# Query products of the second attention: one fp32 matmul each, or three over rounded parts and remainders

## What is computed

```python
# x: [32, 32, 512]; 32 heads, NOPE = ROPE = 64, KVR = 32, VD = 128
q = _rmsnorm(x @ wq_a.T, q_a_ln_w) @ wq_b.T
q_nope, q_pe = (q[..., :NOPE], q[..., NOPE:])
ckv_kpe = x @ wkv_a.T
ckv, k_pe = (ckv_kpe[..., :KVR], ckv_kpe[..., KVR:])
kv = _rmsnorm(ckv, kv_a_ln_w) @ wkv_b.T
k_nope, v = (kv[..., :NOPE], kv[..., NOPE:])
q_pe, k_pe = rope(q_pe), rope(k_pe)
scores = (q_nope . k_nope + q_pe . k_pe) * softmax_scale, causal
out = softmax(scores) @ v @ wo.T
```

## Time and profile before

| what | value |
|---|---|
| median of 3 runs | 1026.8 us (1025.46 to 1026.83) |
| the profiled execution's own time | 1021.81 us |
| span of that execution, first to last instruction | 1019.7 us |
| mean granted TensorE clock | 0.991 |
| PE busy | 966.5 us, 95% of the span |
| DVE, POOL, ACT busy | 554.2, 458.9, 229.2 us |
| second attention's stages and output, about 753 to 910 us | 157 us |

### The profile page before, as it was taken

One profiled execution on the slowest core, in us unless ns is written; L12 is line 12 of the kernel. 1 busy time (PEld: TensorE's weight loads), 2 busy tenths in 40 slices (PEclk: granted clock), 3 DMA queues, 4 the chain that ended last, 5 costly groups with the idle time before them and its releaser, 6 DMA issues.

```text
span 1019.7 us, 15772 instructions
## 1 busy us (share of the span) xinstructions
PE 966.5 (95%) x6686; PEld 695.8 (68%) x6686; DVE 554.2 (54%) x947; ACT 229.2 (22%) x443; POOL 458.9 (45%) x417
## 2 busy tenths in 40 slices
PE   6899989999999999999999789989989999899997
PEld 2338877778888788777887578738845556446853
DVE  7856739475384835648376434434147968302323
ACT  4602022221302212111210200110161655500001
POOL 7935548584675837578275403202112434320300
PEclk9999999999999999999999899999999999999999
DMA  5782102011111011211014092694340000072002
GB/s 136 184 238 67 55 1 79 36 42 53 43 73 42 3 50 42 73 42 53 1 42 124 1 215 86 136 195 161 131 186 1 2 2 3 1 158 70 4 1 83
DMA packets 36286, 74.29 MB, mean 73 GB/s; under 512 B 13492, under 2 KB 22260, under 8 KB 33140
## 3 DMA queue, kind: packets, MB, share of 16 engines
q1 hardware_dynamic: 35880, 72.89, 25.6%
q10 hardware_dynamic: 336, 0.39, 0.1%
HBM read 66.26 MB, written 7.01 MB: 72 GB/s over the span
## 4 chain that ended last, share of the span: by engine, by line
PE 72%; DVE 10%; POOL 7%; DMA 4%; ACT 3%; issue 3%; SPq 1%; POOLq 0%; DVEq 0%; ACTq 0%
PE ps L1133 14%; PE ps L1195 12%; PE ps L994 8%; PE ps L1439 5%; PE ps L1267 5%; PE ps L1372 5%; PE ps L1147 4%; POOL w_lo L2307 3%; DVE arena L1973 3%; DMA arena<-level_rows 2%; ACT acts L1484 2%; DVE arena L1970 2%; PE ps L1393 1%; PE ps L1272 1%; PE ps L1399 1%
## 5 line engine op out<-in xcount | busy, mean ns | idle before, releaser
L2413 POOL TENSOR_TENSOR arena<-arena 128x512 f32<-128x512 f32 x80 | 103.5, 1295 | 123.1 <-DVE arena L1973 123.0
L1133 PE MATMUL ps<-xt_hi,w_hi 128*128 128x512 f32 x320 | 127.9, 400 | 5.8 <-POOL w_lo L2307 2.7
L1133 PE MATMUL ps<-xt_lo,w_hi 128*128 128x512 f32 x320 | 125.6, 392 | 0.0
L1133 PE MATMUL ps<-xt_hi,w_lo 128*128 128x512 f32 x320 | 125.0, 391 | 0.0
L1195 PE MATMUL ps<-h_hi,wo_hi 128*128 128x512 f32 x256 | 104.9, 410 | 11.9 <-DVE h_lo L1982 11.9
L1991 DVE TENSOR_TENSOR fresh<-ps,fresh 128x512 f32<-128x512 f32 x56 | 38.7, 692 | 133.7 <-PE ps L1195 133.6
L1973 DVE TENSOR_TENSOR arena<-ps,rope 64x512 f32<-64x512 f32 x160 | 110.2, 689 | 2.2
L1195 PE MATMUL ps<-h_lo,wo_hi 128*128 128x512 f32 x256 | 103.1, 403 | 0.0
L1195 PE MATMUL ps<-h_hi,wo_lo 128*128 128x512 f32 x256 | 102.3, 400 | 0.0
L2330 POOL TENSOR_TENSOR xt<-arena 128x512 f32<-128x512 f32 x24 | 30.5, 1270 | 137.0 <-DVE arena L1878 137.0
L1577 ACT ACTIVATE h_hi<-ps 128x512 fp32r<-128x512 f32 x64 | 33.0, 603 | 203.1 <-PE ps L1180 203.1
(11 more groups left out here) (313 smaller groups left out, 1804.0 us busy)
## 6 DMA issues: line engine op xcount, KB each, us to landing
acts<-in_w_o_dram SPq DMA_DIRECT2D x8, 1024.0 KB, 4.9
arena<-in_a_wo_dram SPq DMA_DIRECT2D x8, 1024.0 KB, 5.7
arena<-kernel_rows SPq DMA_DIRECT2D x11, 512.0 KB, 11.3
acts<-in_w_qkv_dram SPq DMA_DIRECT2D x3, 1792.0 KB, 7.3
acts<-in_w_qkv_dram SPq DMA_DIRECT2D x4, 1280.0 KB, 6.6
w_l<-kernel_rows SPq DMA_DIRECT2D x10, 512.0 KB, 11.9
arena<-level_rows SPq DMA_DIRECT2D x4, 1024.0 KB, 21.3
stream<-in_x_dram SPq DMA_DIRECT2D x4, 512.0 KB, 6.7
```

Source lines behind the costliest of these rows:

```text
L1133: last = pe.matmul(ps[:, bank, :], w[:, r, cols], x, start=(r == 0 and n == 0), stop=(r == R - 1 and n == 2))
L2413: pool.tensor_tensor(qk[:, chunk, half * HALF:(half + 1) * HALF], rot[:, k % 2, 0, :], rot[:, k % 2, 1, :], ALU.add).then_inc(s_rope, 1)
```

## The change

Only the 80 products of L1372 and L1380 and what feeds them are changed. Query input, latent query weights and rotary query weights are each held as a rounded part (float32r) and a remainder, and each product is made in three float32r matmuls that accumulate in one bank: high x high, high x low, low x high. The product of the two remainders is left out. The rounded parts take the place of the float32 tiles that ACT wrote before (`wql_hi`, `qa_hi`); rotary weights, which came by DMA, are rounded by 8 new ACT copies of 128 x 512 and split by 8 new POOL subtractions; the other remainders are made by 4 new DVE instructions from PSUM. `wq_lo` is written over `wq1`. New waits: PE for the DVE remainders and, at the first tile of a stage, for POOL's split; DVE, POOL for ACT's rounding; ACT, before it copies heads out over the weights' place in stages 4 to 7, for query tiles to be done. No DMA is added or moved; one offset is rounded up to a multiple of 8 elements.

```diff
...
@@ -424,9 +425,11 @@
         wo1_last = att1.take(GQ, R * P)
-        wql = att1.take(2, GQ, 4 * LAT)
+        WQL_AT = att1.at
+        att1.take(2, GQ, 4 * LAT)
         wcomb = att1.take(8, R, P)
-        qa_t = att1.take(TOK)
+        QA_AT = att1.at
+        att1.take(TOK)
         keys_t = att1.take(TOK)
         class Wide(Region):
@@ -452,6 +455,12 @@
+        qa_hi = rounded("qa_hi", [P, TOK], "arena", QA_AT)
+        qa_lo = rounded("qa_lo", [P, TOK], "w_l0", 8 * TOK)
+        wql_hi = rounded("wql_hi", [P, 2, GQ, 4 * LAT], "arena", WQL_AT)
+        wql_lo = rounded("wql_lo", [P, 2, GQ, 4 * LAT], "xt", 3 * TOK)
+        wq_hi = rounded("wq_hi", [P, NH // GQ, GQ * 2 * ROT], "w_l0", sp0.at)
+        wq_lo = rounded("wq_lo", [P, NH // GQ, GQ * 2 * ROT], "arena", 0)
         stage1 = acts[:, 0:R * WPART]
...
@@ -1348,6 +1361,7 @@
                     if m % 4 == 3:
                         last.then_inc(s1_turn, 1)
                 pe.wait_ge(s1_wqc, 2)
+                pe.wait_ge(s1_wqlo, 2)
                 for m in range(NTILE):
                     last = pe.transpose(ps[:, 4 + m // 4, (m % 4) * P:(m % 4 + 1) * P],
                                         lat_n[:, m].rearrange("p k l -> p (k l)"), ident[:, :])
@@ -1365,20 +1379,28 @@
                         pe.wait_ge(left, count)
                     return ring1_at[name]
+                def three(bank, high, low, half):
+                    x_hi, x_lo = (x[:, half * HALF:(half + 1) * HALF] for x in (qa_hi, qa_lo))
+                    pe.matmul(ps[:, bank, :], high, x_hi, start=True, stop=False)
+                    pe.matmul(ps[:, bank, :], high, x_lo, start=False, stop=False)
+                    return pe.matmul(ps[:, bank, :], low, x_hi, start=False, stop=True)
                 def queries(i, tiles):
                     for k in tiles:
                         bank = ring(("q", i, k))
                         g, half = k // 2, k % 2
-                        pe.matmul(ps[:, bank, :], wq1[:, GQ * i + g, :],
-                                  qa_t[:, half * HALF:(half + 1) * HALF], start=True, stop=True).then_inc(s1_q, 1)
+                        cols = slice(g * 2 * ROT, (g + 1) * 2 * ROT)
+                        if k == 0:
+                            pe.wait_ge(s1_wlo, i + 1)
+                        three(bank, wq_hi[:, i, cols], wq_lo[:, i, cols], half).then_inc(s1_q, 1)
                 def latent_queries(four):
                     for n in range(8):
                         bank = ring(("l", four, n))
                         g, half = n // 2, n % 2
-                        pe.matmul(ps[:, bank, :], wql[:, four, g, :],
-                                  qa_t[:, half * HALF:(half + 1) * HALF], start=True, stop=True).then_inc(s1_l, 1)
+                        three(bank, wql_hi[:, four, g, :], wql_lo[:, four, g, :], half).then_inc(s1_l, 1)
                 def scores(i):
                     rows = slice(32 * (i % 4), 32 * (i % 4) + 32)
@@ -1415,6 +1437,7 @@
                         last.then_inc(s1_pv, 1)
                 pe.wait_ge(s1_turnc, 6)
+                pe.wait_ge(s1_qlo, 2)
                 pe.wait_ge(s1_wcc, 8)
                 latent_queries(0)
@@ -1626,7 +1649,7 @@
                 def copy_query_weights(q):
                     act.wait_ge(s1_wq, q + 1)
-                    act.activation(wql[:, q].rearrange("p g (i l) -> p g i l", i=4),
+                    act.activation(wql_hi[:, q].rearrange("p g (i l) -> p g i l", i=4),
                                    ps[:, 4 + q, :].rearrange("p (i g l) -> p g i l", i=4, g=GQ), ACT.Copy).then_inc(s1_wqc, 1)
                 def copy_output_weights(i):
@@ -1648,13 +1671,20 @@
                             .then_inc(s1_root, 1)
                 for q in range(2):
                     act.wait_ge(s1_turn, q + 1)
-                    act.activation(qa_t[:, q * HALF:(q + 1) * HALF], ps[:, q, :], ACT.Copy,
+                    act.activation(qa_hi[:, q * HALF:(q + 1) * HALF], ps[:, q, :], ACT.Copy,
                                    scale=a1_ln[:, 0, 0:1]).then_inc(s1_turnc, 1)
                 for q in range(4):
                     act.wait_ge(s1_turn, q + 3)
                     dst = (keys_t, keys_l)[q // 2]
                     act.activation(dst[:, q % 2 * HALF:(q % 2 + 1) * HALF], ps[:, 2 + q, :], ACT.Copy)\
                         .then_inc(s1_turnc, 1)
+                def round_queries(i):
+                    if i == 0:
+                        act.wait_ge(s1_turn, 6)
+                    act.activation(wq_hi[:, i, :], wq1[:, GQ * i:GQ * (i + 1), :].rearrange("p h n -> p (h n)"), ACT.Copy)\
+                        .then_inc(s1_whi, 1)
                 def latents_in(four):
@@ -1687,13 +1717,20 @@
                     last.then_inc(s1_place, 1)
                 def heads_out(i):
+                    if i >= R:
+                        act.wait_ge(s1_q, 8 * (2 * (i - R) + 2))
                     for half in range(2):
                         act.wait_ge(s1_pv, 2 * i + half + 1)
                         act.activation(latent(i)[:, half * HALF:(half + 1) * HALF], ps[:, HEADS1[half], :],
                                        ACT.Copy).then_inc(s1_head, 1)
+                round_queries(0)
+                round_queries(1)
                 latents_in(0)
                 for i in range(9):
+                    if i + 2 < 8:
+                        round_queries(i + 2)
                     if i:
                         spread(i - 1, 0)
                         spread(i - 1, 1)
@@ -2190,6 +2227,16 @@
                 ch.link(dve.tensor_tensor(values1, values1, a1_ln[:, 0, 1:1 + LAT].unsqueeze(1)
                                           .broadcast_to([P, NTILE, LAT]), ALU.mult))
                 dve.tensor_copy(lat_n, values1.unsqueeze(2).broadcast_to([P, NTILE, G, LAT])).then_inc(s1_kn, 1)
+                for q in range(2):
+                    dve.wait_ge(s1_wqc, q + 1)
+                    src = ps[:, 4 + q, :].rearrange("p (i g l) -> p g i l", i=4, g=GQ)
+                    split = [w[:, q].rearrange("p g (i l) -> p g i l", i=4) for w in (wql_hi, wql_lo)]
+                    dve.tensor_tensor(split[1], src, split[0].bitcast(F32), ALU.subtract).then_inc(s1_wqlo, 1)
+                for q in range(2):
+                    dve.wait_ge(s1_turnc, q + 1)
+                    cols = slice(q * HALF, (q + 1) * HALF)
+                    dve.scalar_tensor_tensor(qa_lo[:, cols], ps[:, q, :], a1_ln[:, 0, 0:1], qa_hi[:, cols].bitcast(F32),
+                                             ALU.mult, ALU.subtract).then_inc(s1_qlo, 1)
                 def rotate(i, k):
                     dve.wait_ge(s1_q, 8 * i + k + 1)
@@ -2397,8 +2444,17 @@
                 pool.memset(made, 0.0).then_inc(s1_zero, 1)
                 pool.wait_ge(s1_zero, 1)
+                def split_queries(i):
+                    pool.wait_ge(s1_whi, i + 1)
+                    pool.tensor_tensor(wq_lo[:, i, :], wq1[:, GQ * i:GQ * (i + 1), :].rearrange("p h n -> p (h n)"),
+                                       wq_hi[:, i, :].bitcast(F32), ALU.subtract).then_inc(s1_wlo, 1)
+                split_queries(0)
+                split_queries(1)
                 for i in range(8):
                     p = probs1[:, i % 2]
+                    if i + 2 < 8:
+                        split_queries(i + 2)
                     soft_mask(i, SOFT0, p)
                     soft_shift(i, SOFT0, p, stat1, (0,))
                     soft_scale(i, SOFT0, p, stat1)
```

More of the change, by code:

```diff
@@ L299, in build @@
         f1_bias = sp0.take(1, R)
+        sp0.at = -(-sp0.at // 8) * 8
         sp1 = Spare()
@@ L583, in build @@
         s1_zero = sem("l1_zeros_made")
+        s1_whi = sem("l1_query_weights_rounded")
+        s1_wlo = sem("l1_query_weights_split")
+        s1_qlo = sem("l1_query_inputs_split")
+        s1_wqlo = sem("l1_absorbed_query_split")
         s1_q = sem("l1_query_tile_done")
```

## The result

The changed kernel takes **1012.9 us** (median of 4 runs, 1012.35 to 1013.29) against 1026.8 for the kernel before on the same chip (4 runs, 1025.46 to 1027.14): a ratio of 0.987, 95% interval 0.9845 to 0.9895. It is 13.9 us faster; 10.5 had been forecast, and the range held the time. The profiled execution took 1012.35 us with a span of 1010.6, where that of the kernel before took 1021.81 with 1019.7.

What follows compares the result with a forecast made beforehand. TensorE was taken to bound the kernel, DVE close behind. Gains and losses 4.1 + 0.8 + 4.1 + 1.5 + 0.4 - 0.2 - 0.2 = 10.5 us, off 1026.8, gave 1016.3 us; range 1011.5 to 1022.5.

Steps and rivals of the forecast that it cites:

- The bound: Whole kernel and second attention: TensorE busy for 95% of the span; in stage 4 DVE only 1.8 us behind it.
- The pace: The 80 query products: passes 0.229 us apart, a product 0.686 instead of 0.858, saving 0.172 each.
- the first 24 products: Start of the second attention: 24 x 0.172 = 4.1 us gained, neither DVE's rotates nor ACT's copies being slower.
- Stages 1, 2 and 4: Full stages of eight products: 4.1 us gained, PE's work 11.83 us a stage, DVE 0.4 short of it.
- Stage 0 and stage 5: Stages where PE waits on DVE's chain: 0.8 us gained of 1.4 in stage 0, 0.4 of 1.4 in stage 5.
- Stage 3: Stage with 16 products: 1.5 us gained of 2.7, after a new 1.2 us wait for ACT's latent copy.
- Head and POOL: 0.2 us lost before the first product to DVE's subtractions; 0.2 lost to POOL's added instructions beside DVE.
- (a): Rival: TensorE's clock falls in new waits of stages 0 and 3, costing up to 3.4 us; 1019.7 us, chance 0.11.
- (b): Rival: DVE becomes the bound, each POOL split lengthening its work by 1.287 us; 4.5 gained, 1022.3 us, chance 0.09.
- (c): Rival: every product restarts the array after its ring wait, 8.8 us lost; gain 1.7, 1025.1 us, chance 0.05.
- (d): Rival: three weight loads per product stand in the open, 25 us slower, 1052 us; chance 0.05 together with (e).
- (e): Rival: a float32r matmul is split in two records again, 6 in place of 2, slower; chance 0.05 with (d).

Runs made afterwards that it cites:

- the kernels with two, three and four of them: Changed kernel without its middle pass, 1009.3 us; changed kernel itself, 1012.9 us; changed kernel with the product of the two remainders added, 1031.5 us.
- the two-pass kernel: The pass of rounded weights with the query input's remainder left out of the changed kernel: 1009.3 us, 5.5 less than the changed kernel.
- all three traces of the changed kernel: The changed kernel profiled three times with no edit; medians 1012.9, 1014.8 and 1014.8 us, against 1026.8, 1026.2 and 1024.5 for the kernel before.
- the second execution: Profiled execution of the changed kernel run again, nothing edited: median 1014.8 us against 1026.2 for the kernel before, ratio 0.9895.

## Why the prediction was right, step by step

**The bound.** Right: TensorE paces the full stages, before and after. One reading was off: the clock line has one slice below 9, not two, and a 9 means 90% or more, not full speed. Nothing in the sum used it.

**The pace.** Right: 0.231 from start to start instead of 0.229, the product 0.693 against 0.686. Over 80 products that is 0.6 us, and it is where the 0.2 each of the first 24 products and of stages 1, 2 and 4 went. The passes of a new form were priced from the same form elsewhere in the program, and the kernels with two, three and four of them bear the price out. The rule of "FP8 and Floating Point Precision" in the Trainium skill (TensorE Precision Notes), three of a float32 product's four passes, gives an estimate of 0.643 for a product; the trace has 0.693.

**Stages 1, 2 and 4.** Right: 11.9 us against 11.83, PE without idle time, DVE 11.3 to 11.5 busy. That DVE was 0.4 to 0.6 us short of PE and no more is what the two-pass kernel showed by stopping at 11.20 to 11.25. POOL had more room than forecast: after the split it still waited 1.7 us for DVE's pull (forecast 0.3 to spare), so its wait of 2.99 us shrank by the split alone.

**Stage 0 and stage 5.** Right in mechanism and size (0.65 of 0.8, 0.35 of 0.4): DVE's chain from the end of the scores sets them, and only what DVE had idled for PE could go. The wait for the third rotate rose from 0.22 to 0.88. The second half of `pv(5)`, which DVE's chain and the spread release, starts 15.13 us after stage 5 begins, where it was 15.46: 0.3 gained, in all three traces of the changed kernel. The 0.35 of the whole row depends on the clock as well: in the second execution, where the fall comes later, that row gained 0.8. The wait of about 2 us before `pv(5)` came as 0.58 and 1.49, one before each half.

**Stage 3.** Right in mechanism; the wait was a little too long in the forecast. The spread ended 3.2 us into the stage, as worked out, and the bank was free at 815.23, 3.83 in (forecast 3.9). PE wanted it at 4 x 0.693 and 0.11 for the restart of the first pass, 2.88 in, instead of 2.7, so it came 0.95 late, not 1.2 (the row's 0.77 is less because the modelled end of the record before lies later than the next start). The slower passes take back what the shorter wait gave: 1.6 gained for 1.5. That the copy behind the spread is the cause was shown by moving it to DVE, which took 1.05 us off the stage: the 0.95 and the restart.

**Head and POOL.** These two terms were mis-sized, at 0.2 each: both measured nothing. The head took 4.96 us for 4.95. The added subtractions did make PE's transposes of the latents later, by 0.14 us, but the forecast had this delay reach the last of ACT's four copies, and it did not: the four took 2.06 us in a row as before, and the last ended where it had.

```profile
752.22 1.28 DVE L2234 TENSOR_TENSOR wql_lo<-ps,wql_hi 128x512 fp32r<-128x512 f32 x2
753.55 2.06 ACT L1679 ACTIVATE arena<-ps 128x512 f32<-128x512 f32 x4
753.64 1.06 PE L1366 MATMUL ps<-ident,w_l 128*128 128x128 f32 x8
```

POOL beside DVE cost nothing, which was the lower bound. The price of 0.25 us for a shift beside POOL was misread: the shifts of 0.80 and of 1.05 both wait for POOL (above), and the transposes beside the splits are not of that kind.

**The rivals.** (a), the clock in the new waits of stages 0 and 3, did not come in the changed kernel, but with a wait of 2.97 us it did (two passes). Behind the part, where the forecast had not looked, the first output records ran at the lower clock in two of the three executions, which took 1.5 and 2.6 us of the gain: in one after a wait of 2.08 us, where the kernel before waits 1.36, in the other the clock had been low since `pv(6)`. Whether the change brings this about or chance, three traces against two don't show. (b) fell with the splits taken out. (c), a restart per product, is excluded by 11.90 us stages. (d) and (e): passes of 0.231 leave no room for loads of 190 ns in the open, and every pass has one record.

**From sum to median.** The sum, 10.5, met the part's 10.4. To a tenth this is luck: the gains had been put 0.5 us too high and the two losses 0.4 too high. The changed kernel's profiled execution took 1012.35 us for 1011.3 forecast. The median came out 3.4 us below the forecast, because I added the whole distance between one profiled execution of the kernel before and its median (5.0 us) to the changed kernel, whose own profiled execution lay 0.5 us from its median. That distance belongs to executions, not to kernels: those of the kernel before spread over 8 us, with their clock. So the median lay in the range, 1.4 us from its lower end, by a gain that was right and an offset that was not. What decides in an execution where the clock falls stays open.

## What to carry to other kernels

When the leading engine's instruction gets cheaper, work out for each stage how far the second engine lies behind, and count the gain only down to there: here 10.4 of 13.2 us came through (80 x 0.165 by the measured pace), and one pass less brought only a third of its price. Price a new form by a row of the same form elsewhere in the program, from start to start. When the scatter of executions is as large as the effect, compare the same stretch in two traces, and follow it far enough to see what its end hands on. Then look at what the gain exposes: work that is ready, put into waits that end in a lower clock, brought another 6.4 us here.

## What the hardware showed that I had not expected

- The same wait does not always cost the same clock. After 2.12 us of idle time ahead of the output the first eight records took 3.67 us, which is full clock, after 2.08 in another execution of the same program 6.30; before, 1.36 us had no fall behind it. Two executions with the same 1.49 us before `pv(5)` had the fall in one and full clock in the other.
- A wait that leads to the lower clock costs about itself once more: from start to start, the two groups behind the 1.49 us took 3.52 us, and 1.90 in the execution without the fall.
- The first pass after a wait takes 0.34 us to the next start, not 0.23, and its record has 0.50 instead of 0.39; with one such wait in stage 0 and one in stage 3 this is 0.1 us each. The wait is not needed for it: the first pass after `scores` or `pv`, where PE never stood still, has the same 0.50 and 0.33.

```profile
787.57 0.50 PE L1385 MATMUL ps<-qa_hi,wq_hi 128*128 128x512 f32 x1
787.90 0.39 PE L1386 MATMUL ps<-qa_lo,wq_hi 128*128 128x512 f32 x1
```

- DVE's shift, with two inputs in SBUF, ends 0.54 to 0.56 us behind POOL's shift however long the two overlap (0.25 or 0.5 us); its transposes run beside POOL's subtractions at 690 ns, and at 693 without them.
